# Fused graph attention: TensorE signals with an empty drain behind its matmuls in place of the matmuls' own increments

## The reference, cut to what matters

```python
h = (x @ W).reshape(-1, H, C)                       # 4 heads of 64
e = leaky_relu(alpha_s[src] + alpha_d[dst], 0.2)    # a score for each edge and head
m = segment_max(e, dst)
ex = exp(e - m[dst])
s = segment_sum(ex, dst)
alpha = ex / (s[dst] + 1e-16)
out = segment_sum(h[src] * alpha[:, :, None], dst)  # weighted sum of the neighbours' rows
```

## Time and profile before

| | value |
|---|---|
| median of 3 timed runs | 7405.83 us |
| lowest and highest of them | 7404.95 and 7408.0 us |
| span of the profiled execution | 8931.6 us |
| the three `attend` stretches in it | 1054 to 2514, 2698 to 4149, 7508 to 8891 us |
| busy share of the span | GpSimd 65%, TensorE 61%, VectorE 56%, ScalarE 43% |

### The profile page before, as it was taken

One profiled execution on the slowest core, in us unless ns is written; L12 is line 12 of the kernel. 1 busy time (PEld: TensorE's weight loads), 2 busy tenths in 40 slices (PEclk: granted clock), 3 DMA queues, 4 the chain that ended last, 5 costly groups with the idle time before them and its releaser, 6 DMA issues. The chain is left out here.

```text
span 8931.6 us, 130458 instructions
## 1 busy us (share of the span) xinstructions
PE 5412.5 (61%) x23088; PEld 4000.6 (45%) x23089; DVE 4963.7 (56%) x11653; ACT 3871.5 (43%) x9075; POOL 5847.5 (65%) x8186
## 2 busy tenths in 40 slices
PE   6442365666535656664676666658888754666665
PEld 5431244444424444443455555435555533444443
DVE  6444355555545555554677777744444445555556
ACT  2220255455424554552244444335555533454444
POOL 0555677777747777775467666657777765777774
PEclk9555677777767777776788988868888866777777
DMA  4112233333313333331466666423333323333332
GB/s 143 49 49 52 75 95 95 95 96 95 86 44 97 96 95 95 96 97 33 127 176 178 177 176 175 129 64 99 100 101 100 101 53 101 99 99 99 98 98 74
DMA packets 580940, 894.72 MB, mean 100 GB/s; under 512 B 307359, under 2 KB 357708, under 8 KB 580448
## 3 DMA queue, kind: packets, MB, share of 16 engines
q0 software_dynamic: 245984, 649.30, 26.7%
q1 hardware_dynamic: 334448, 218.84, 8.9%
q10 hardware_dynamic: 416, 25.60, 0.9%
HBM read 859.36 MB, written 59.47 MB: 103 GB/s over the span
## 5 line engine op out<-in xcount | busy, mean ns | idle before, releaser
L2002 POOL DMA_INDIRECT ad_ring<-tab_qv,ad_idx x808 | 770.7, 954 | 506.4 <-issue 217.6
L1515 POOL DMA_INDIRECT at_ring_0a<-tab_s,at_idx_0a x808 | 774.3, 958 | 430.9 <-PE at_po_0a L1680 219.2
L2396 POOL DMA_INDIRECT ae_ring<-tab_a,ae_idx x808 | 777.9, 963 | 423.0 <-PE ae_po L2553 233.7
L1515 POOL DMA_INDIRECT at_ring_0b<-tab_s,at_idx_0b x808 | 772.8, 956 | 426.7 <-PE at_po_0b L1680 213.2
L1515 POOL DMA_INDIRECT at_ring<-tab_s,at_idx x808 | 780.1, 965 | 377.6 <-PE at_po L1680 183.0
L1680 PE MATMUL at_po_0a<-at_rows_0a,at_hot_0a 128*128 128x264 f32 x1616 | 625.6, 560 | 520.8 <-ACT at_hr_0a L1780 199.8
L1680 PE MATMUL at_po_0b<-at_rows_0b,at_hot_0b 128*128 128x264 f32 x1616 | 624.3, 559 | 512.2 <-ACT at_hr_0b L1780 201.7
L1680 PE MATMUL at_po<-at_rows,at_hot 128*128 128x260 f32 x1616 | 614.5, 553 | 444.5 <-DVE acc L1566 179.0
L1680 PEld LDWEIGHTS at_po_0a<-at_rows_0a,at_hot_0a 128*128 128x128 f32 x1616 | 439.3, 282 | 670.8 <-DVE acc L1566 262.0
L1680 PEld LDWEIGHTS at_po_0b<-at_rows_0b,at_hot_0b 128*128 128x128 f32 x1616 | 438.5, 282 | 662.4 <-DVE acc L1566 264.4
L1680 PEld LDWEIGHTS at_po<-at_rows,at_hot 128*128 128x128 f32 x1616 | 435.9, 280 | 586.2 <-DVE acc L1566 225.4
(11 more groups left out here) (508 smaller groups left out, 14085.4 us busy)
## 6 DMA issues: line engine op xcount, KB each, us to landing
at_rr_0a<-relrow_d SPq DMA_DIRECT2D x102, 256.0 KB
at_rr_0b<-relrow_d SPq DMA_DIRECT2D x102, 256.0 KB
ad_rr<-relrow_d SPq DMA_DIRECT2D x102, 256.0 KB
at_rr<-relrow_s SPq DMA_DIRECT2D x102, 256.0 KB
ae_feat<-attr_pad SPq DMA_DIRECT2D x808, 32.0 KB
rnk_lrow<-lorow_f SPq DMA_DIRECT2D x98, 256.0 KB
attr_pad<-in_edge_attr_dram ACTq DMA_DIRECT2D x1, 25000.0 KB, 79.1
at_ring_0a<-tab_s,at_idx_0a POOLq DMA_INDIRECT x808
```

What stands on the lines that cost most here:

```text
L1515: eng.indirect_dma_start(out=ring[:, t.slot * STEP + u, :], out_offset=None, in_=table, in_offset=bass.IndirectOffsetOnAxis(ap=idx[:, t.sl ...
L2002: eng.indirect_dma_start(out=ring[:, t.slot * STEP + u, :], out_offset=None, in_=table, in_offset=bass.IndirectOffsetOnAxis(ap=idx[:, t.sl ...
L2396: eng.indirect_dma_start(out=ring[:, k, :], out_offset=None, in_=table, in_offset=bass.IndirectOffsetOnAxis(ap=idx[:, k:k + 1], axis=0))\
```

## The change

Every signal of TensorE inside `attend` moves from the matmul to an empty `drain` instruction behind it. For the sums there is one drain behind each second matmul: `mm0`, `mm2`, ... skip their increment, and the drain behind `mm1`, `mm3`, ... adds two. Nothing else changes: not the waits, not the order of the matmuls, not the other kernels.

```diff
-                                m.did(f"mm{u}", eng.matmul(po[:, u % 4, 0:W], hot[:, q % 2, j, :],
-                                                           rows[:, q % 2, j, :, :].rearrange("p h f -> p (h f)"),
-                                                           start=True, stop=True))
+                                eng.matmul(po[:, u % 4, 0:W], hot[:, q % 2, j, :],
+                                           rows[:, q % 2, j, :, :].rearrange("p h f -> p (h f)"), start=True, stop=True)
+                                if j % 2:
+                                    m.did(f"mm{u}", eng.drain())
+                                else:
+                                    m.skip(f"mm{u}")
...
-                                mm = eng.matmul(pb[:, u, :, :].rearrange("p k c -> p (k c)"),
...
-                            m.did(f"spread{h}", mm)
+                            m.did(f"spread{h}", eng.drain())
...
-                            m.did("scores", eng.transpose(scores_in, picked[:, :, :].rearrange("p h u -> p (h u)"), ident[:, :]))
+                            eng.transpose(scores_in, picked[:, :, :].rearrange("p h u -> p (h u)"), ident[:, :])
+                            m.did("scores", eng.drain())
...
-                            m.did("back_turned", eng.matmul(pe[:, KX * R:KX * R + H],
-                                                            expd[:, EX:EX + 1].to_broadcast([R, P]), ident[0:R, 0:R:STEP],
-                                                            start=True, stop=True))
+                            eng.matmul(pe[:, KX * R:KX * R + H], expd[:, EX:EX + 1].to_broadcast([R, P]),
+                                       ident[0:R, 0:R:STEP], start=True, stop=True)
+                            m.did("back_turned", eng.drain())
...
-                            m.did("joined", mm)
+                            m.did("joined", eng.drain())
```

More of the change, by code:

```diff
@@ L1691, in spread @@
                                 u = h * HALF + k
-                                mm = eng.matmul(pb[:, u, :, :].rearrange("p k c -> p (k c)"),
-                                                hot_r[:, h, k * P:(k + 1) * P],
-                                                b_tab[:, bass.ds(gs[u], 1), :, 0:C].rearrange("p o k c -> p (o k) c"),
-                                                start=True, stop=True)
-                            m.did(f"spread{h}", mm)
+                                eng.matmul(pb[:, u, :, :].rearrange("p k c -> p (k c)"),
+                                           hot_r[:, h, k * P:(k + 1) * P],
+                                           b_tab[:, bass.ds(gs[u], 1), :, 0:C].rearrange("p o k c -> p (o k) c"),
+                                           start=True, stop=True)
+                            m.did(f"spread{h}", eng.drain())
                         if scores:
@@ L1734, in step @@
                             for k in range(3):
-                                mm = eng.matmul(joined[0:C * STEP, :], parts[:, k, :, :].rearrange("p c u -> p (c u)"),
-                                                ident[:, :], start=(k == 0), stop=(k == 2))
-                            m.did("joined", mm)
+                                eng.matmul(joined[0:C * STEP, :], parts[:, k, :, :].rearrange("p c u -> p (c u)"),
+                                           ident[:, :], start=(k == 0), stop=(k == 2))
+                            m.did("joined", eng.drain())
                         else:
```

## The result

The changed kernel takes 8447.31 us (median of 4 runs, 8445.43 to 8452.16), the kernel before beside it 7405.39 us. The ratio is 1.141, 95% interval [1.139, 1.143]: 1042 us slower, 6.8 us for each of the 153 turns. The forecast was 7560 us with a range to 7800: the sign was right, the size was not.

What follows compares the result with a forecast made beforehand. Waits between engines bound it: a timed turn of 23.8 us, above GpSimd's 23.1. Terms 0.8 + 1.1 + 0.5 + 0.4 + 0.35 + 0.45 = 3.6 lift the ring to 24.8: 153 x 1.0 = +153 us, predicted 7560 us, range 7150 to 7800.

Steps and rivals of the forecast that it cites:

- the lateness: In a turn of attend, TensorE's matmul increments come late while gathers run: 7.5 us a turn in the profiled execution.
- the choice on which the forecast rested: Late time mostly exists only with the profiler on; the timed kernel has at most 0.7 us a turn to win.
- The rival of late increments in the timed runs: Late matmul increments are in the timed runs too, so the change is faster: 7222 us if half are there; chance 0.36.
- the signs of prompt signals: Changed profile: own within 0.2 us of joined's end, alphas within 0.3 of back_turned, TensorE idle over 1.3 before spread.
- the step of the slack: Timed turn of 23.8 us less ring of 21.2 leaves 2.6 us a turn; drains cost in full only beyond it.
- The 21.2 us: Length of the ring VectorE, TensorE, ScalarE with signals on time, read from the last turn between two exponentials.
- Pairs inside `mm4` to `mm11`: Three drains with a matmul behind, 0.35 to 0.45 us each, partly hidden by VectorE's adds: +0.8 us a turn.
- The drain behind `mm11` and the load: Ahead of spread, the queue cannot run ahead, so TensorE's register load stands open: +1.1 us a turn (0.75 to 1.3).
- `spread0`, `spread1` and `back_turned`: Their drains between the register load and mm12: +0.5 us for spread0 and spread1, +0.4 us for back_turned, a turn.
- The drains behind `mm13` and `mm15`: In the last sums and adds of a turn: +0.35 us behind mm13, +0.45 us behind mm15.
- each keeps a fixed duration: 386 ns, 951 ns: Instructions keep fixed durations, so waits, not instructions, explain the profiled span of 8931.6 us against the timed 7405.83 us.
- estimate of 32 us of gain from fewer increments: 13 increments instead of 21 a turn, 26.3 ns each: 0.2 us a turn, which would make the forecast 7527 us.

Runs made afterwards that it cites:

- e_other_drains: The kernel before with only the five drains of scores, spread0, spread1, back_turned and joined; the sums keep their own increments: 7577.9 us, ratio 1.024.
- e_fill_pause_load: The kernel before with 20 unawaited matmuls and TensorE's register load ahead of mm4, and GpSimd's memset of 128 instead of 256 columns: 7073.48 us, ratio 0.955.
- e_after_fill_load: The changed kernel with TensorE's register load and 20 matmuls that nobody waits for, both placed ahead of mm4: 7835.01 us.
- e_sum_drains: The kernel before with only the eight drains behind pairs of sums; all other signals stay on the matmuls: 8378.82 us, ratio 1.129.
- e_before_again: The kernel before, unchanged, profiled a second time: 7400.83 us, profiled span 7397.0 us.
- The runs with fillers: 20 matmuls that nobody waits for, in TensorE's idle time ahead of mm4: 7333.99 us on the kernel before, 8181.93 us on the changed kernel.
- e_pair_incs: The kernel before with sums signalled in pairs by the second matmul's own increment, without a drain: 7503.01 us, ratio 1.013.

## Why the prediction was right and wrong

**Right: the lateness does not exist in the timed runs.** This was the choice on which the forecast rested. The timed turn was put at 28.75 x 0.829 = 23.8 us, and it is 23.8, 23.8 and 23.3. The stages outside `attend` did shrink as well (first exponential at 854.7 us in place of 1030.8). The second profile belongs to one of the timed runs (7398.81 us), so it speaks for them. That all stages shrink alike was an assumption, and it came out: the three passes went to 0.82 of the first profile, the rest to 0.83. The rival of late increments in the timed runs, with its 0.36, is refuted by the second profile.

**Right: the mechanism and the signs of prompt signals.** `own` starts 0.06 us behind the end of `joined` (1329.26 against 1329.20), `alphas` 0.06 behind `back_turned`, and TensorE is idle for 1.69 us before `spread`, over the 1.3 named. But a turn is 30.5 us, not 24 to 25.5, and GpSimd's waits did not fall below 2 us: in the turn shown they are 3.85 + 1.72.

**Wrong, the step of the slack: "the slack 23.8 - 21.2 = 2.6 us between ring and turn".** The 21.2 us came from one turn, and in that turn `mm12` to `mm15` took 2.02 us (8860.28 to 8862.30), all at 2.4 GHz. The same last turn in the second profile (its timeline) takes 7337.30 - 7314.69 = 22.6 us:

```profile
7314.69 0.31 ACT L1796 ACTIVATE at_exp<-at_less 64x129 f32<-64x129 f32 x1 [1.53 <-DVE at_less L1639]
...
7324.65 3.42 PE L1680 MATMUL at_po<-at_rows,at_hot 128*128 128x260 f32 x8
...
7337.30 0.31 ACT L1796 ACTIVATE at_exp<-at_less 64x129 f32<-64x129 f32 x1 [2.14 <-DVE at_less L1639]
```

with 3.42 us for these four matmuls, at 1.2 GHz for most of them. In the passes, turns of about 22.8 us stand beside turns of over 24 (exponentials at 1164.25, 1188.69, 1211.54, 1236.56 and 1259.39 us: 24.4, 22.9, 25.0 and 22.8). The last stretch tells them apart: 4.09, 2.73, 4.42 and 2.73 us in these four. So the timed turn of 23.8 us was the ring itself, at a mix of the two clocks. In the first two passes there was no slack, in the third about 0.5 us (23.3 against 22.7 with a halved pause). `e_other_drains` shows it: 0.99 us more on the ring, 1.2 us a turn more. This step is worth up to 2.6 x 153 = 398 of the 887 us by which the forecast was too low.

**Wrong, the terms of the sum.** The kind of each cost was named; two sizes were too small, two were about right:

- Pairs inside `mm4` to `mm11`, +0.8 in the sum. At one and the same clock, 2.4 GHz, eight sums take 3.72 us without drains (`e_fill_pause_load`) and 1310.84 + 1.15 - 1306.55 = 5.44 with (`e_after_fill_load`): 1.72 us for three drains, 0.57 each. The prediction had 0.35 to 0.45 each and let VectorE's adds hide nearly half. They hid none; in the turn shown, one of the three stops is even longer by a wait for an add (0.40 us in place of 0.21).
- The drain behind `mm11` and the load, +1.1: measured 1.86. Only the load's own duration was counted; the drain's stop of 0.43 us and the 0.16 us of overlap that was there before come on top.
- `spread0`, `spread1` and `back_turned`, +0.9: measured 0.99 in `e_other_drains`, so about right. In the changed kernel the stretch grew by 1.26 us, but with the sums' drains alone (`e_sum_drains`) it had already grown by 0.29, at the lower clock.
- The drains behind `mm13` and `mm15`, +0.8: measured 0.91, about right in the sum. The parts were not: 0.56 for the stops, where 0.35 was said, and 0.35 for the later signals, where 0.45 was said.

Together 5.48 us in place of 3.6, 1.88 us or 288 us of the time.

**Missing: the clock.** The sum held every matmul at its duration, and the prediction says why: "each keeps a fixed duration: 386 ns, 951 ns". Its own has matmul records of 386 ns at the least and 647 at the median, the two clocks side by side. The rest of the measured 6.88 us a turn, 6.88 - 5.48 = 1.4 us, has no term in it. The means of the first pass show where it is: of `mm4` to `mm11` 0.1 us, of `spread` to `mm12` 0.4 and of `mm12` to the last add 1.89 - 0.91 = 1.0 are not the drains' own. There `mm12` to `mm15` took 4.2 us or more in all 49 turns, mostly or wholly at 1.2 GHz, where 22 of 49 had run at 2.4 and taken 2.05. The granted clock of the first pass fell from 0.80 to 0.70 (windows of after: `e_before_again` has 0.80 in the same stretch):

```profile
1200.00:1600.00 400.00, 262.65 (x949) 160.31 (x949) 208.90 (x507) 189.18 (x442) 266.12 (x417) 0.70 0.33 89
```

The runs with fillers point the same way: they bring the distance between the two kernels from 1042 down to 8181.93 - 7333.99 = 848 us, 1.3 us a turn, although GpSimd stops the gain of the kernel before and the first pass of the changed one comes back to 0.78 only. The stops are idle time of TensorE on the ring, more of the matmuls behind them run at 1.2 GHz, and these make the ring longer again. For a single stop that need not hold: behind `mm5` alone, fewer ran at 1.2 GHz than before. Slack, terms and clock give 2.6 + 1.88 + 1.4 = 5.88 us a turn, 900 us, against the 887 missing. This sum closes by construction, since the clock's 1.4 us is what the terms leave over.

**What the drain and the fillers bear out.** The trace shows `spread` idle for 1.69 us behind a drain, 0.43 us with the load moved. The Trainium skill (PSUM — Partial Sum Buffer, Engine vs sequencer instructions) says to put the increment on the matmul itself and that a drain waits for the engine to go fully idle; the trace agrees, and only a run gave the price. The granted clock is 0.91 with fillers against 0.80 without. The Trainium skill (TensorE: Matmul & The Clock Gate, What's actually happening) says that the lower clock is the default and that activity lifts it; the trace agrees. The prediction's estimate of 32 us of gain from fewer increments goes back to the Trainium skill (TensorE: Matmul & The Clock Gate, The cost: per-tile semaphore tail), whose figure of 26.3 ns for each increment was fitted on small matmuls that share the array. No run here shows such a gain: `e_pair_incs` has eight increments fewer a turn and is 95 us slower, but it also tells VectorE later of the first sum, so it does not measure the figure either.

**What stays open.** Why the first profiled execution of before had TensorE's increments late, and others of the same program not. It was not confined to `attend`: ahead of the first pass VectorE's L442, which waits for TensorE's `rnk_got`, was idle for 231.8 us there and for 0.8 in the second profile. That run cannot be repeated. And what part of the last 762 us between `e_fill_pause_load` and `e_after_fill_load` (which also has the full pause) is clock at `mm12` to `mm15`: at most 1.84 x 153 = 282 us.

## What to carry to other kernels

Let the instruction that makes the data carry the signal. An empty drain costs little where nothing on the path stands behind it, as here behind `scores` and `joined`. In mid-stream it costs 0.3 to 0.6 us of overlap, and it lays open whatever the queue was running ahead with, here a register load of 1.1 us. Before believing an effect that a profile shows and that the timed runs should share, compare its span with the timed median; if they differ by 20%, profile again before reasoning from it. Where a ring of engines sets the pace and TensorE idles in it, its matmuls have two durations: price a change at both, and look for idle time to fill, which here gave 68 us by itself and, with an early load and a shorter pause, 331. And before a timed turn less a ring is called slack, check at which of the two durations the ring was read.

## What was not expected of the hardware

- One empty instruction a turn behind `mm11` cost 436 us, 5.9%, and 229 us with fillers, which keep the clock up; the same instruction behind `mm5` cost 30 us.
- One profiled execution was 21% longer than the timed runs of the same program (8931.6 against 7400), with TensorE's increments late in it, and the next was 7397.0.
- A stop behind a drain shows as 0.21 us of idle time between two pairs of fp32 matmuls at either clock (1.15 or 2.12 us a pair), and as 0.43 us in front of the bf16 `spread`.
